# x's rows in memory 128 KB apart in place of 64 KB, in a conditioned residual kernel on one core

## The reference

```
w = weights[conditions]                       # (64, 64, 64)
return x + jnp.einsum('bct,bcd->bdt', x, w)   # x: (64, 64, 512)
```

## Time and profile before

| what | value |
|---|---|
| median of 3 runs | 46.07 us (46.05 to 46.08) |
| the profiled execution's own time | 45.89 us |
| its span, first to last instruction | 44.6 us |
| TensorE (PE) busy | 30.4 us, 68% of the span |
| VectorE (DVE) busy | 15.1 us, 34% |
| ScalarE (ACT) busy | 13.4 us, 30% |
| GpSimd (POOL) busy | 1.7 us, 4% |
| read from and written to HBM | 9.44 MB and 8.39 MB, 400 GB/s over the span |

### The profile page before, as it was taken

How to read it: one execution, slowest core, us unless ns; L and a number is a source line. 1 busy time by engine, 2 the same in 40 slices (tenths; PEclk the granted TensorE clock), 3 DMA queues, 4 the chain that set the end, 5 groups by cost and what they waited for, 6 DMA issues and landing times.

```text
span 44.6 us, 331 instructions
## 1 busy us (share of the span) xinstructions
PE 30.4 (68%) x100; PEld 13.1 (29%) x100; DVE 15.1 (34%) x24; ACT 13.4 (30%) x16; POOL 1.7 (4%) x9
## 2 busy tenths in 40 slices
PE   0040000699999479999999799999999999920000
PEld 0040000425333054542443234435344353300000
DVE  1310000000019980857730590095086073073000
ACT  0894000000000073835710580094085071072000
POOL 4009000000000000000000000000000000000000
PEclk9999999999999999999999999999999999999995
DMA  0679999999999999999995989999899999999994
GB/s 0 110 301 419 419 426 419 434 441 419 434 426 426 500 470 470 470 470 470 470 441 220 397 382 441 470 456 441 382 397 419 411 441 426 419 434 419 404 426 169
DMA packets 1730, 17.83 MB, mean 400 GB/s; under 512 B 194, under 2 KB 194, under 8 KB 194
## 3 DMA queue, kind: packets, MB, share of 16 engines
q1 hardware_dynamic: 1584, 16.78, 89.6%
q0 software_dynamic: 144, 1.05, 5.6%
q10 hardware_dynamic: 2, 0.00, 0.0%
HBM read 9.44 MB, written 8.39 MB: 400 GB/s over the span
## 4 chain that ended last, share of the span: by engine, by line
DMA 50%; PE 31%; SPq 4%; DVE 3%; issue 1%; POOLq 0%
DMA x_sb<-x 50%; PE product L166 31%; SPq L94 4%; DVE y_sb L216 3%; POOLq L134 0%
## 5 line engine op out<-in xcount | busy, mean ns | idle before, releaser
L166 PE MATMUL product<-x_sb,w_diag 128*128 (+1 forms) x40 | 17.7, 598 | 0.3 <-POOLq L134 0.3
L216 DVE COPY y_sb<-product 128x1024 f32<-128x1024 f32 x8 | 9.8, 1224 | 12.8 <-PE product L166 10.5
L117 ACT COPY y_sb<-product 128x1024 f32<-128x1024 f32 x8 | 8.1, 1014 | 13.6 <-PE product L166 11.3
L166 PEld LDWEIGHTS product<-x_sb,w_diag 128*128 128x128 f32 x40 | 7.4, 190 | 10.5 <-issue 10.5
L146 PE MATMUL product<-x_sb 128*128 128x512 f32 x10 | 6.7, 841 | 5.3 <-DMA x_sb<-x 5.3
L158 PE MATMUL product<-x_sb,w_all 64*64 64x512 f32 x48 | 5.5, 600 | 0.9 <-DVE w_all L205 0.9
L146 PEld LDWEIGHTS product<-x_sb 128*128 128x128 f32 x10 | 2.6, 275 | 8.6 <-issue 8.6
L111 ACT COPY w_diag<-w_all 64x256 f32<-64x256 f32 x1 | 0.6, 637 | 12.1 <-DVE w_all L205 12.1
L202 DVE TENSOR_TENSOR gathered<-gathered,piece 128x64 f32<-128x64 f32 x1 | 0.3, 267 | 10.1 <-DMA gathered<-weights,table_row 10.1
L158 PEld LDWEIGHTS product<-x_sb,w_all 64*64 64x64 f32 x48 | 2.5, 200 | 3.9 <-issue 2.1
L205 DVE STREAM_TRANSPOSE w_all<-gathered 128x2048 f32<-128x2048 f32 x1 | 2.3, 2311 | 0.0
(11 more groups left out here) (9 smaller groups left out, 1.6 us busy)
## 6 DMA issues: line engine op xcount, KB each, us to landing
x_sb<-x SPq DMA_DIRECT2D x4, 1024.0 KB, 9.0
x_sb<-x SPq DMA_DIRECT2D x1, 4096.0 KB, 22.4
out<-y_sb SPq DMA_DIRECT2D x2, 2048.0 KB, 7.9
out<-y_sb SPq DMA_DIRECT2D x4, 1024.0 KB, 5.4
condition<-conditions ACTq DMA_DIRECT2D x1, 0.2 KB
gathered<-weights,table_row POOLq DMA_INDIRECT x1, 9.7
```

What stands on the lines that cost most here:

```text
L117: nc.scalar.copy(y_sb[:, 4 * turn:4 * turn + 2, :], product[turn % SETS][0][:, :, :]).then_inc(moved_by_act, 1)
L166: product_of = nc.tensor.matmul(product[s][j][:, g, :], w_diag[:, s, 2 * j + g, :], x_pair(2 * j + g), start=True, stop=True)
L216: nc.vector.tensor_copy(y_sb[:, 4 * turn + 2:4 * turn + 4, :], product[turn % SETS][1][:, :, :]).then_inc(moved_by_dve, 1)
```

## The change

The host makes `x_laid` twice as long per row: 64 pairs of which the first 32 hold data and the others zeros. The kernel is given the first 32. Its input tensor grows from 8.39 MB to 16.78 MB, and a row begins every 128 KB. What the kernel reads of each row, and the result's tensor, are as before. No line of the program on the chip differs, and each engine's instructions stand in the same order and number; what differs is the step between rows in the addresses of the five loads of `x`, and where the tensors lie in memory.

```diff
-    x_laid = np.asarray(x).reshape(B // PAIR, PAIR, C, T).transpose(1, 2, 0, 3).reshape(PAIR * C, B // PAIR, T)
+    x_laid = np.zeros((PAIR * C, B, T), np.asarray(x).dtype)
+    x_laid[:, :B // PAIR] = np.asarray(x).reshape(B // PAIR, PAIR, C, T).transpose(1, 2, 0, 3).reshape(PAIR * C, B // PAIR, T)
...
-    conditioned_residual_kernel(nc, *args, out[:, :B // PAIR, :])
+    conditioned_residual_kernel(nc, args[0][:, :B // PAIR, :], *args[1:], out[:, :B // PAIR, :])
```

## The result

The changed kernel takes 46.31 us (median of 22 runs) against 46.05 us for the kernel before on the same chip (22 runs). The ratio is 1.005 with a 95% interval of 1.003 to 1.007, so it is slower by half a per cent. The ratios leave out single executions far above the rest, here one of the changed kernel's 22 at 48.04 us. The forecast was 46.07 us and no change. The profiled execution of the changed kernel took 46.16 us, 0.27 us more than that of before (45.89), with a span of 44.9 us against 44.6.

The account below looks back on a forecast made before the run. The prediction took DMA traffic of 17.83 MB to nearly fill the span, with a second path of load, matmuls, copy and last store ending together with it. All terms were 0 us, so the median stayed 46.07 us, range 45.8 to 46.8.

Parts of the forecast that it names:

- What bounds the kernel: Whole span: 17.83 MB of DMA traffic nearly fills it, 44.26 of 44.6 us; later loads move the end one for one.
- two paths end together: End of span: the traffic as such, and load, matmuls, copy, last store, both end there, the second at 44.56 us.
- Issue, compute, bytes at 0 us: SyncE's queue, compute and x's padding: same instructions and 17.83 MB, padding never read, so 0 us each.
- Both directions meet one ceiling: Steady reads and stores: 428 and 425 GB/s at DMA share 1.01 and 1.00, so something common sets the rate.
- The Trainium skill's 3% at that pitch: Loads of x: skill page's loss for HBM-to-HBM copies at 512 KiB pitch; on x alone it would give about +0.6 us.
- The term of 0 us for the reads: Loads of x: rows 128 KB apart read as fast as rows 64 KB apart; 0 us, between -0.7 and +0.9.
- the only slower ramp considered: Loads of x: the ramp's 236 GB/s held for all of x, +16 us; left out of the range.
- The rival on the slower side: Reads from 3.2 to 25.1 us fall under the ceiling; at 410 GB/s +0.86 us, 46.9 us; chance 0.27.
- its smaller case: Reads of x: half the loss priced at 410 GB/s, giving 46.5 us; within the slower rival's chance of 0.27.
- Its point of decision: Reads of x: slower rival decides once their rate falls under about 426 GB/s, 0.09 us in 19.6.
- The signs named for "right": Profile after: 428 GB/s from 3.20 to 13.20 us, x ends 25.1, gather's wait 13.2, TensorE idle 0.3 us before turn 4.
- the prediction's 512 KB and 1 MB between rows read together: Reads of x: assuming 128 rows shared out in blocks of 8, rows read together stand 512 KB apart before, 1 MB after.

Follow-up runs that it names:

- the two kernels with copies: Each of the five loads reads its own copy of x, rows 128 or 64 KB apart: 46.23 us and 46.08 us, kernel before 46.09.
- the packed head: The change, but turn 0's 1 MB comes from a tensor of its own with rows 8 KB apart: 46.19 us, ratio 1.0028 to the kernel before.
- The near head with the far tail: Turns 0 to 3 loaded from rows 64 KB apart, the 4 MB load from rows 128 KB apart: 45.95 us, ratio 0.9986 to the kernel before.
- the four kernels: Against the kernel before: long tensor with rows 64 KB apart, and rows 68, 132 and 256 KB apart; ratios 1.0006, 1.0007, 1.0014, 1.0017.

## Why the prediction was wrong

- **What bounds the kernel: right.** The traffic nearly fills the span, and a lag in it moves the end: 0.10 MB, 0.24 us, against 0.27 measured between the two profiles. One for one holds over all the profiles (0.020 us per packet), not for each pair of them. That two paths end together holds too, and the two kernels with copies show that the last store's issue can be earlier and the end later.
- **Issue, compute, bytes at 0 us: right**, but for a trifle. The loop takes 14.01 us in both, the padding is not read (17.83 MB, 1730 packets in both). The five issues take 2.56 us in place of 2.49.
- **Both directions meet one ceiling, and the steady reads don't slow: right.** 425 GB/s against 428 here, 428 and 429 for the change on two other chips, and 424 and 426 with rows 512 KB apart. The sign was 428 within 1 or 2, which the 425 of the first profile just misses. The Trainium skill's 3% at that pitch (page "DMA: Bandwidth & Descriptors", section "Latency and other measured facts") is not seen in the steady rate. What half a per cent there is comes from elsewhere; that page's figures are of copies within HBM, which no run here makes.
- **The term of 0 us for the reads: the step that failed.** It was taken from the steady row and put on all reads, the first ones too. The text treated the ramp only as a place where time could be gained, and held that it "has little to do with the distance between rows, since each engine is then at its first rows". The runs show the reverse: the ramp is where the distance acts. It measured 236 GB/s before and 195 after, and the term 0.24 us in place of 0. The range of 45.8 to 46.8 us does hold 46.31, but it was made for other reasons: its slower side priced a loss in the steady reads (410 GB/s), and the only slower ramp considered was one that lasts for all of x (16 us).
- **The rival on the slower side** had the right sign, and 0.26 us came where its smaller case has 0.43 (46.5 us), but at the wrong place, so that is luck. It wanted 410 to 424 GB/s in the steady reads, and the loss is not there. Its point of decision, 426 GB/s for x, was no use either. What decides is the bytes of the first 3 us.
- **The signs named for "right"** show the miss as well: the gather's wait ended at 13.46, not 13.2 us, and the load at 25.25, not 25.1. TensorE's idle time before turn 4 shrank to 0.22 us, since the gather, and with it turn 3, was later by more than the load.

Why distant rows make the first packets slow is open. That a power of two is all of it is unlikely (1.0014, 1.0020 and 1.0024 without one), but not ruled out. Distance alone is not ruled out either: the counts on chip 2 fall with it, and the packed head, whose rows are 8 KB apart, had its 29 packets with idle engines and not with slow packets. Against it stand 30 packets at 128 KB beside 35 at 132, and 29 beside 32 at 512, from single executions. What counts may be which addresses the 16 engines ask for together at the start, but this was only argued, not tested: nothing here moved the engines' starting rows against each other with the rest left alone. Nor does a run show how the rows are shared out among the engines, so the prediction's 512 KB and 1 MB between rows read together stay an assumption.

No version beat the kernel before by more than the scatter. The near head with the far tail came to 0.9986 with an interval up to 1.0008.

## What to carry to other kernels

Where transfers fill the span, look at the first few microseconds as a stage of their own, and count bytes from the start, not rates in the middle: what the ramp doesn't move is paid for at the end at about the price of plain traffic. A row of the steady state says nothing about the ramp. Here only the loads issued first needed care: the later half of x could be read from rows 128 KB apart without a cost that can be seen. And compare single profiles on one chip only; the same count of packets can mean a slow ramp on one and a usual one on another.

## What was not expected of the hardware

- The steady reads run at 423 to 429 GB/s with rows 64, 68, 128, 132, 256, 512 and 516 KB apart, from 3.20 to 13.20 us.
- Before that most profiles have a gap between about 2.2 and 2.8 us in which few packets begin, after each engine's first. From 1.60 to 2.20 us the kernel before moves 205 GB/s and the changed one 192, nearly the same; from 2.20 to 2.80 us 177 and 41 (82 in both later profiles of the change). On chip 2 the four kernels show 232 to 314 GB/s there. In the kernel before, the slices from 1.6 to 4 us (0.06 us each) run through it and recover; in the changed kernel they stay low for longer:

```profile
GB/s 4 0 273 410 273 273 546 137 0 137 137 0 137 0 0 0 410 410 410 273 410 410 546 273 137 546 410 683 410 137 546 410 683 137 410 546 137 819 137 546
```

```profile
GB/s 4 0 137 546 0 819 0 137 273 0 0 0 0 137 0 0 137 0 137 0 546 546 410 137 273 683 546 410 273 137 546 546 410 273 410 546 546 410 137 410
```

- A packed first load of 1 MB, which lies in one piece, moves as little as the change by 3 us (29 packets), though with idle engines (share 0.24) and not with longer packets.
